# Ternary layers of a four-block transformer kernel: chunk 1's activations copied behind the next unit's first seed, and their low part behind statistics, in the slots without down projections

## What is computed

```python
def _L1_ffn_ref(x, gate_w, up_w, down_w, gate_s, up_s, down_s):   # gate_w, up_w: 1408 x 512 of -1, 0, 1
    xf = x.reshape(b * s, h)
    g = jnp.einsum('th,ih->ti', xf, gate_w) * gate_s
    u = jnp.einsum('th,ih->ti', xf, up_w) * up_s
    hdn = jax.nn.silu(g) * u
    out = jnp.einsum('ti,hi->th', hdn, down_w) * down_s
    return out.reshape(b, s, -1)
...
x = x + 0.5 * _L1_ffn_ref(_layernorm(x, axis=-1), ...)            # ternary, before the state space
x = x + _L1_attn_ref(_layernorm(x, axis=-1), ...)                 # state space
x = x + 0.5 * _L1_ffn_ref(_layernorm(x, axis=-1), ...)            # ternary, after it
```

## Time and profile before

| | us |
|---|---|
| median of 3 runs | 1729.14 |
| lowest, highest | 1728.69, 1729.4 |
| the profiled execution | 1728.94 |
| its span, first to last instruction | 1727.1 |
| TensorE busy | 1705.9 |
| VectorE busy | 1156.4 |
| ScalarE busy | 825.3 |

### The profile page before, as it was taken

One profiled execution on the slowest core, in us unless ns is written; L12 is line 12 of the kernel. 1 busy time (PEld: TensorE's weight loads), 2 busy tenths in 40 slices (PEclk: granted clock), 3 DMA queues, 4 the chain that ended last, 5 costly groups with the idle time before them and its releaser, 6 DMA issues. The chain is left out here.

```text
span 1727.1 us, 21358 instructions
## 1 busy us (share of the span) xinstructions
PE 1705.9 (99%) x7696; PEld 1391.7 (81%) x7696; DVE 1156.4 (67%) x1802; ACT 825.3 (48%) x1350; POOL 128.3 (7%) x188
## 2 busy tenths in 40 slices
PE   8999999999999999999999999999999999999998
PEld 6778888888888888888888888888787777787786
DVE  8977678677775655754446554456668769767866
ACT  5744544455575543434223333223556455655534
POOL 1000000000012220000000000000000235100001
PEclk9999999999999999999999999999999999999999
DMA  9775555699985000344345344443656651366655
GB/s 332 263 281 219 216 193 189 253 357 364 374 334 203 1 1 1 110 165 164 142 149 194 119 165 162 150 148 143 242 221 241 230 217 76 134 227 228 233 219 220
DMA packets 76235, 340.33 MB, mean 197 GB/s; under 512 B 7904, under 2 KB 18528, under 8 KB 70496
## 3 DMA queue, kind: packets, MB, share of 16 engines
q1 hardware_dynamic: 76128, 338.93, 52.4%
HBM read 259.73 MB, written 79.17 MB: 196 GB/s over the span
## 5 line engine op out<-in xcount | busy, mean ns | idle before, releaser
L512 PE MATMUL psum<-xc_hi,w 128*128 128x512 f32 x1544 | 610.3, 395 | 2.7 <-ACT psum L1260 1.1
L514 PE MATMUL psum<-xc_lo,w 128*128 128x512 f32 x1544 | 602.2, 390 | 0.0
L516 PE MATMUL psum<-xc_hi,w 128*128 128x512 f32 x928 | 361.3, 389 | 0.0
L512 PEld LDWEIGHTS psum<-xc_hi,w 128*128 128x128 f32 x1544 | 289.7, 188 | 85.8 <-ACT psum L1260 12.0
L512 PE MATMUL psum<-w,hid 128*128 128x512 f32 x864 | 338.4, 392 | 2.9 <-DVE x L2171 1.8
L516 PE MATMUL psum<-w,hid 128*128 128x512 f32 x864 | 336.6, 390 | 0.0
L514 PEld LDWEIGHTS psum<-xc_lo,w 128*128 128x128 f32 x1544 | 290.1, 188 | 56.1
L1903 DVE TENSOR_TENSOR x<-psum,x 128x512 f32<-128x512 f32 x256 | 173.1, 687 | 148.5 <-PE psum L516 148.3
L514 PE MATMUL psum<-w,hid 128*128 128x512 f32 x544 | 211.8, 389 | 0.0
L1927 DVE TENSOR_TENSOR hid<-sg,hid 128x512 fp32r<-128x512 f32 x216 | 149.5, 702 | 91.9 <-ACT hid L1279 87.0
L516 PEld LDWEIGHTS psum<-xc_hi,w 128*128 128x128 f32 x928 | 174.2, 188 | 36.6
(11 more groups left out here) (163 smaller groups left out, 2016.6 us busy)
## 6 DMA issues: line engine op xcount, KB each, us to landing
w<-w_kept SPq DMA_DIRECT2D x186, 896.0 KB, 6.5
w<-w_kept SPq DMA_DIRECT2D x94, 512.0 KB, 7.5
w_kept<-w SPq DMA_DIRECT2D x16, 1792.0 KB, 7.6
w_kept<-prep SPq DMA_DIRECT2D x12, 1792.0 KB, 7.8
w_kept<-w SPq DMA_DIRECT2D x16, 512.0 KB, 6.4
w_kept<-prep SPq DMA_DIRECT2D x12, 512.0 KB, 8.7
att_raw<-in_att_w SPq DMA_DIRECT2D x4, 1024.0 KB, 8.9
x<-in_x SPq DMA_DIRECT2D x4, 1024.0 KB, 11.6
```

Source lines behind the costliest of these rows:

```text
L512: pe.matmul(out, a_hi, b_hi, start=start, stop=False, skip_group_check=onto)
L514: last = pe.matmul(out, a_hi, b_lo, start=False, stop=stop and zero == "a", skip_group_check=onto)
L516: last = pe.matmul(out, a_lo, b_hi, start=False, stop=stop, skip_group_check=onto)
```

## The change

In the three open slots of each ternary pass, ScalarE copies the high part of chunk 1 behind the next unit's `seed_y` instead of at the end of the slot before, ahead of the seed. On VectorE, in the slot ahead of an open one, `hid_low(u, 1)` and the `extra` operation behind it change places.

```diff
@@ ScalarE: ternary_slot
                 seed_y(u)
-                if s and s not in ps.open:
+                if s in ps.open:
+                    hid_high(u - 1, 1)
+                elif s:
                     hid_high(u - 1, 0)
                     hid_high(u - 1, 1)
                 keep_p5(u)
...
                 if s == ps.n - 2:
                     seed(ps, 7)
-                if s + 1 in ps.open:
-                    hid_high(u, 1)
@@ VectorE: ternary_slot
                 elif s + 1 in ps.open:
+                    extra(ps, s, 2)
                     hid_low(u, 1)
-                    extra(ps, s, 2)
```

## The result

| | kernel before | changed kernel |
|---|---|---|
| median, us | 1729.27 (6 runs, 1728.69 to 1730.65) | 1736.75 (6 runs, 1736.33 to 1737.85) |
| ratio | | 1.0042, 95% interval 1.0032 to 1.0052 |
| profiled execution, its span | 1728.94, 1727.1 | 1736.73, 1734.9 |

The change makes the kernel 7.5 us slower, clear of the noise. The page of the changed kernel shows where: TensorE does the same work, and its idle time is named. Busy lines first, then the granted clock, then two groups (busy us, mean ns | idle time ahead of it and what ended most of it); the first two lines and the clock answer to the earlier trace rows.

A forecast was written before the change was run, and what follows sets the result against it. TensorE, busy 99% of the span, was taken to bound the kernel, so only delays to matmuls cost time. Delays of p7 at 12 places sum to 7.6 us on 1729.14, forecasting 1736.7 us, range 1733.3 to 1738.8.

The forecast's parts named there:

- The chain: At the changed slots: first seed, high part, low part, keeping p5, z seed, p7 follow in sequence; p7 0.61 us later.
- T: Start of the last matmul of p1 in a changed slot, from which the prediction counts its times.
- The first seed's gain: Ahead of p6: the first seed starts 0.15 us earlier, about 0.16 comes back per place, 1.9 us over 12 places.
- a late weight load: In p2's start, from which the gap ahead of p7 was counted: a delay of 0.1 us, gap about 0.95.
- What comes behind p7: Rest of each changed slot: all moves by the same 0.60 us, nothing is given back, each of 12 places pays anew.
- (b): Unit 10 of two passes: a sum of 1.22 us lies between low part and z seed; 0.83 us each.
- (c): Unit 1 of the pass behind the state space: gating was late already, so p7 is only 0.41 us later.
- (a): Unit 2 of the first ternary pass: statistics and aggregates ahead of the low part add 0.12 us, making 0.72.
- The sum: All 12 places: 8 x 0.60 + 0.72 + 2 x 0.83 + 0.41 = 7.6 us slower.
- The regular eight: The eight places outside the special ones: p7 later by 0.60 us each.
- The clock: Rival: pauses of 0.95 us at 12 places drop TensorE to 1.2 GHz, 76 us more, 1813 us; 1%.
- VectorE's queue: Rival: low part behind statistics, sum and z seed in one queue costs some 2 us more, 1738.8 us; 5%.

The follow-up runs named there:

- second tile: Changed kernel with kept p5 going alternately to one of two tiles in the ternary passes: 1728.44 us, ratio 0.9994; the kernel before with that tile: 1728.17 us, ratio 0.9990.
- doubled low part: Changed kernel with the low part of chunk 1 computed twice in sequence at the 12 places: 1746.39 us, ratio 1.0095 to the kernel before.

## Why the prediction was right, point by point

**The chain.** Every link came as worked out: seed T+0.43, high part T+0.92, low part T+1.57, p5 kept T+2.36, z seed T+3.05, p7 T+3.81, within 0.02 at the nine places without aggregates or a sum. The links were taken from unit 3, which had the same two operations in the same order; the kept wait was read in the bracket of the earlier trace rows. The second tile shows that this wait is the cause, and the doubled low part that the chain has no slack.

**The first seed's gain.** It came, 2.3 us of weight-load waits against 1.9 forecast, and was swallowed by the wait ahead of p7. With the chain cut it is there: p7 0.15 to 0.21 earlier at nine places with the second tile. One size was off without changing the sum: a late weight load was put at 0.1 us and cost 0.04, so p2's last matmul starts at T+2.77 and not T+2.83, and the gap ahead of p7 is 1.03 to 1.06 us and not 0.95.

**What comes behind p7.** The second half of the unit keeps its 2.9 us in both kernels; nothing was given back, and each place paid for itself, as the run with unit 10 alone shows.

**The special places.** (b) 0.83 forecast, 0.82 twice. (c) 0.41 forecast and measured. (a) 0.72 forecast, 0.58 measured, and here a term was mis-sized: the low part followed the start of the aggregates by 0.29, not by their whole 0.38, and was late against its due time by 0.06, of which p7 saw 0.03. And p7 had stood at T+3.25 here before, not at T+3.20, so that the regular part was 0.55 and not 0.60. The changed kernel's VectorE at this place:

```profile
1218.41 0.68 DVE L1800 BATCH_NORM_STATS2 stats<-x 128x6 f32<-128x512 f32 x1
...
1219.13 0.38 DVE L1804 BATCH_NORM_AGGREGATE meanvar<-stats 128x2 f32<-128x6 f32 x4
1219.42 0.66 DVE L1927 TENSOR_TENSOR hid<-sg,hid 128x512 fp32r<-128x512 f32 x1
```

**The sum.** 7.6 us forecast, 7.24 at the places. The regular eight had been given 0.60; they paid 0.55 to 0.60, since p7 had been at T+3.22 to T+3.25 at six of the eight in the kernel before, and at T+3.20 only in unit 1 of passes 5 and 7. The span grew by 7.8. Of the rest 0.25 us lie between p7 of unit 10 in pass 5 and T of unit 1 in pass 6: 78.57 us against 78.32. This is not plain scatter. The two profiles with the queues of the kernel before (its own and the one with the second tile) have 78.28 and 78.32; all nine with any edit to the order have 78.5 to 78.6. They part at one meeting in the state space, 31.1 us behind that p7. Where GpSimd's product (L1720) starts 0.03 us ahead of VectorE's low part, two low parts in a row take 1.8 us each; where the two start within 0.01 us of each other or VectorE is first, the first low part takes 0.68, and the second 1.8. How an edit elsewhere tips this, and how it ends in 0.25 us, was not followed. Some 0.3 us lie behind the last matmul, in the output's DMAs (6.1 to 6.4 us; 5.6 to 6.6 in the experiments' profiles). That the median hit the forecast to 0.1 us is luck at that size; the twelve places are not.

**The rivals.** The clock stayed in the top tenth in all slices, with pauses of 1.0 to 1.3 us at twelve places. The rule on micro-idling in the Trainium skill (TensorE: Matmul & The Clock Gate) stands there in the section A second HAM failure mode: psum-queue depth-cycling, behind the one that the prediction names, and is told of another kernel; it did not show in this trace. VectorE's queue did not cost more than the sum. What the prediction did not see is how tight the second chain is, silu and seed of W behind the low part of chunk 0. It is in its own rows (the silu 0.78 behind that low part), and cost two experiments their expectation. Nor did it look at what keeping p5 waits for outside the twelve places; that wait cost 0.95 us in pass 5 already in the kernel before.

## What to carry to other kernels

A copy moved behind an urgent one may still stand in a chain of its own: before moving it, list who waits for what it frees, not only for what it makes, and add up start-to-start distances until TensorE. Where two users share a tile, the second waits for the slowest reader of the first; one more tile (2 KiB per partition here) took the loss away, and with a sum moved too the same reordering gained 2.3 us at the places where it had lost 7.2. Filler work on a queue is free only while the operation behind it has nothing late to wait for.

## What was not expected of the hardware

Start-to-start distances between engines repeat to 0.01 to 0.03 us over the twelve places and all kernels run here (where nothing else stood between): 0.65 from the high part's start to the low part's, 0.78 from the low part's to the copy that waits for it, 0.69 on to the z seed, 0.76 on to the matmul. A row of four aggregates, 0.38 us long, frees VectorE for its next operation after 0.29. In eleven profiles, a start of a GpSimd operation 0.03 us ahead of VectorE's went with two VectorE operations of 1.8 us, and any later start with one of 0.68 and one of 1.8. The median of the kernel before lay between 1729.27 and 1730.05 us from one batch of runs to the next, as much as some of these edits move, so effects of 1 us were read from the profile by place and not from the medians.
